# A fused graph, attention and expert kernel on one core: tiles and superchunks taken from the last to the first, x and its table moved tile by tile, two buffer sets for the permutation

## The reference, cut to what matters

```python
xn = layernorm(x)                                   # x: 6250 x 256
def sage(h, Wl, bl, Wr):
    agg = segment_sum(h[src], dst)                  # 100000 edges, dst sorted
    return agg / max(count(dst), 1) @ Wl.T + bl + h @ Wr.T
g   = sage(relu(sage(xn, W1l, b1, W1r)), W2l, b2, W2r)
x   = x + g + mix(xn)                               # linear attention over all nodes, two layer norms, a two-layer MLP
H   = gelu(layernorm(x) @ fW1 + fb1)                # 1024 wide
p   = softmax(H @ Wg + bg); e = argmax(p)           # 8 experts, top 1
out = x + p[e] * (H @ Wd[e] + bd[e])
```

## Time and profile before

| what | value |
|---|---|
| median of 3 runs | 2529.69 us (2522.98 to 2529.9) |
| the profiled execution's own time | 2532.22 us |
| its span | 2530.2 us |
| mean granted TensorE clock | 0.877 |
| busy PE, DVE, ACT, POOL | 77%, 45%, 22%, 66% |
| HBM traffic | 332.56 MB, mean 131 GB/s |

### The profile page before, as it was taken

One profiled execution on the slowest core, in us unless ns is written; L12 is line 12 of the kernel. 1 busy time (PEld: TensorE's weight loads), 2 busy tenths in 40 slices (PEclk: granted clock), 3 DMA queues, 4 the chain that ended last, 5 costly groups with the idle time before them and its releaser, 6 DMA issues.

```text
span 2530.2 us, 41380 instructions
## 1 busy us (share of the span) xinstructions
PE 1958.9 (77%) x9589; PEld 1205.7 (48%) x9590; DVE 1138.0 (45%) x3192; ACT 560.1 (22%) x1269; POOL 1673.8 (66%) x1749
## 2 busy tenths in 40 slices
PE   3566778878888898994344666778899999779998
PEld 1234445445555565662011233444455555468886
DVE  5522323347677777773212233334445555432222
ACT  6433334332222222220000000111122222201110
POOL 2677777777777777726777777777777776044442
PEclk9988888889899999997555677888999999889999
DMA  5444444444444444423343444445455544235551
GB/s 181 139 116 117 116 117 120 120 129 131 130 131 137 131 132 133 135 67 110 102 122 106 141 128 140 142 143 156 153 160 156 156 153 144 81 120 164 169 163 67
DMA packets 154316, 332.56 MB, mean 131 GB/s; under 512 B 34181, under 2 KB 88423, under 8 KB 154245
## 3 DMA queue, kind: packets, MB, share of 16 engines
q0 software_dynamic: 85824, 248.21, 33.6%
q10 hardware_dynamic: 42630, 58.35, 6.6%
q1 hardware_dynamic: 25794, 25.32, 3.1%
HBM read 273.97 MB, written 58.72 MB: 131 GB/s over the span
## 4 chain that ended last, share of the span: by engine, by line
POOL 34%; PE 33%; issue 15%; DMA 6%; DVE 4%; ACT 2%; POOLq 2%; ACTq 1%; DVEq 1%; SPq 1%
POOL big L647 34%; PE bank L517 10%; PE bank L1617 8%; PE bank L1387 6%; DMA mbuf<-qT_d 4%; PE bank L1605 2%; PE bank L1393 2%; PE bank L1542 1%; PE bank L1417 1%; PE bank L1484 1%; DMA big<-hh_d,edges 1%; POOLq L644 1%; PE bank L1412 1%; POOLq L642 1%; ACT big L1174 1%
## 5 line engine op out<-in xcount | busy, mean ns | idle before, releaser
L647 POOL DMA_INDIRECT big<-hh_d,edges x782 | 750.2, 959 | 291.1 <-issue 231.8
L647 POOL DMA_INDIRECT big<-xh_d,edges x782 | 771.7, 987 | 246.4 <-issue 234.0
L1387 PE MATMUL bank<-big,S 128*128 x1960 | 599.2, 431 | 267.0 <-SPq L583 260.5
L791 DVE SCALAR_TENSOR_TENSOR S<-edges,tv,iota 128x512 f16<-128x512 f16 x490 | 359.7, 752 | 480.8 <-PE bank L1387 349.8
L1387 PEld LDWEIGHTS bank<-big,S 128*128 128x128 f16 x1960 | 205.0, 105 | 559.7 <-issue 419.6
L1385 PE MATMUL bank<-ones,S 128*128 128x1 f16 x980 | 167.5, 171 | 109.8 <-SPq L583 107.9
L517 PE MATMUL bank<-turned,x1T 128*128 128x512 f32 x392 | 195.4, 621 | 0.0
L1385 PEld LDWEIGHTS bank<-ones,S 128*128 128x128 f16 x980 | 96.1, 98 | 126.2 <-SPq L583 120.6
L667 POOL DMA_INDIRECT out_dram<-big,node_s x56 | 57.0, 1018 | 145.5 <-DVE big L1123 145.5
L517 PE MATMUL bank<-turned,mbuf 128*128 128x512 f32 x196 | 110.5, 693 | 0.0
L517 PEld LDWEIGHTS bank<-turned,abuf 128*128 128x128 f32 x784 | 96.8, 195 | 24.0 <-issue 23.0
(11 more groups left out here) (217 smaller groups left out, 2936.0 us busy)
## 6 DMA issues: line engine op xcount, KB each, us to landing
hx_d<-mbuf ACTq DMA_DIRECT2D x49, 512.0 KB
big<-xh_d,edges POOLq DMA_INDIRECT x782
big<-hh_d,edges POOLq DMA_INDIRECT x782
big<-in_fwd_dram SPq DMA_DIRECT2D x8, 1024.0 KB
qT_d<-abuf ACTq DMA_DIRECT2D x49, 128.0 KB
hh_d<-HL ACTq DMA_DIRECT2D x49, 128.0 KB
mbuf<-qT_d ACTq DMA_DIRECT2D x49, 128.0 KB
hx_d<-res ACTq DMA_DIRECT2D x49, 128.0 KB
```

Of the source, the lines that this page charges most:

```text
L647: e.indirect_dma_start(G[:, r, n % SC, :], None, table, bass.IndirectOffsetOnAxis(ap=srcx[:, n:n + 1], axis=0)).then_inc(d_g[r], 16)
L791: VI.done(e.scalar_tensor_tensor(S[:, walk.u, :, :], dst[:, bass.ds(c * SC, SC)].unsqueeze(2).to_broadcast([P, SC, P]), tv[:, bass.ds(k, 1 ...
L1387: ins = e.matmul(AGG[:], S[:, walk.u, j, :], G[:, bass.ds(slot, 1), j, :].rearrange("p a c -> p (a c)"), start=False, stop=False, skip_gro ...
```

## The change

All tiles are handled from the last to the first: tile t of the program is now nodes (48 - t) * 128 onward (`rows`), superchunk c is now chunks (196 - c) * 4 onward, so superchunk 0 has no chunks, superchunk 1 has two, and the others four. The tables of items and `free_words`, the masks and every load and store of tiles follow. Items 0 to 97 now hold 28 finishes and 70 superchunks, items 98 to 244 hold 21 finishes and 127 superchunks (counted from the inputs). x is loaded tile by tile (49 loads; that of the partial tile waits for three GpSimd clears instead of one), and `xh_d` is stored tile by tile (49 stores instead of 21). GpSimd clears two pieces of the ring more, VectorE clears `xnS` once. The permutation's loop is written out, has two sets of `OL` and `RH` (the second `OL` lies in S), VectorE writes the tile part before the row part, and waits for TensorE's sum of two groups before.

```diff
+def rows(t):
+    return slice((TILES - 1 - t) * P, (TILES - t) * P)
...
-        OL = Gf[:, 0:GROUP * P].rearrange("p (t r) -> p t r", r=P)
-        RH = Gf[:, GROUP * P:GROUP * (P + 3 * SLOTS)].rearrange("p (t k s) -> p t k s", k=3, s=SLOTS)
+        OLS = [a[:, 0:GROUP * P].rearrange("p (t r) -> p t r", r=P)
+               for a in (Gf, S.rearrange("p a b c -> p (a b c)").bitcast(F32))]
+        RHS = [Gf[:, GROUP * (P + n * 3 * SLOTS):GROUP * (P + (n + 1) * 3 * SLOTS)].rearrange("p (t k s) -> p t k s", k=3, s=SLOTS)
+               for n in range(2)]
...
-        X_IN = 32
+        X_IN = 16 * GROUP
...
-        VP = Loop(sem("v_perm"), [x + h for h in "01" for x in ("row", "tile")])
+        VP = Loop(sem("v_perm"), [x + h for h in "01" for x in ("tile", "row")])
...
-                return self.kept((self.k + self.u - self.t) % 256, SUPER - 1)
+                return self.kept((self.t + (SUPER - 1 - self.u) - self.k) % 256, SUPER - 1)
...
-            return range(c * SC, min((c + 1) * SC, CHUNKS))
+            first = (SUPER - 1 - c) * SC
+            return range(min(first, CHUNKS), min(first + SC, CHUNKS))
...
+                for t in (*range(g * GROUP + 1, (g + 1) * GROUP), g * GROUP):
+                    if t > 0:
+                        e.dma_start(res[:, t, :], x[rows(t), :]).then_inc(d_x[g], 16)
+                    else:
+                        e.wait_ge(p_setup, 3)
+                        e.dma_start(res[0:LAST_ROWS, t, :], x[(TILES - 1) * P:N, :]).then_inc(d_x[g], 16)
...
-                    at = slice(g * (GROUP * P) + a * P, g * (GROUP * P) + b * P)
-                    e.dma_start(xh_d[at, :].rearrange("(t p) c -> p t c", p=P), xhl[:, a:b, :]).then_inc(d_xst[n], 16)
+                    for u in range(a, b):
+                        e.dma_start(xh_d[rows(g * GROUP + u), :], xhl[:, u, :]).then_inc(d_xst[n], 16)
...
-            e.memset(res[:, TILES - 1, :], 0.0).then_inc(p_setup, 1)
+            e.memset(res[:, 0, :], 0.0).then_inc(p_setup, 1)
+            for c in range(2):
+                rest = G[:, ring(0, c), len(chunks(c)):, :]
+                e.memset(rest.bitcast(F32), 0.0).then_inc(p_setup, 1)
...
+            step(e.memset(xnS, 0.0))
...
-                    if not first:
-                        PP.wait(e, f"sum{h}", g, 1)
+                    if g > 1:
+                        PP.wait(e, f"sum{h}", g, 2)
+                    VP.done(e.tensor_tensor(RH[:, a:b, 2, :], numbers(SLOTS), of(nv, SLOTS), ALU.is_equal), f"tile{h}")
                     VP.done(e.tensor_tensor(OL[:, a:b, :], numbers(P), of(mx, P), ALU.is_equal), f"row{h}")
-                    VP.done(e.tensor_tensor(RH[:, a:b, 2, :], numbers(SLOTS), of(nv, SLOTS), ALU.is_equal), f"tile{h}")
```

More of the change, by code:

```diff
@@ L581, in relay @@
             def relay(layer, c):
-                e.wait_ge(d_g[ring(layer, c)], landed(layer, c))
+                if landed(layer, c):
+                    e.wait_ge(d_g[ring(layer, c)], landed(layer, c))
                 e.sem_inc(s_ready, 1)
@@ L651, in _ @@
             e.wait_ge(d_sth, OPENED + 16 * TILES)
-            with e.Fori(0, TILES // GROUP) as g:
+            for g in range(TILES // GROUP):
+                RH = RHS[g % 2]
                 for h, (a, b) in enumerate(HALVES):
@@ L726, in moments @@
             def moments(g):
-                e.wait_ge(d_x[g], 32)
+                e.wait_ge(d_x[g], X_IN)
                 for i in range(g * GROUP, (g + 1) * GROUP):
@@ L1084, in _ @@
             rt(e.scalar_tensor_tensor(mx[:], nv[:], -float(P), mx[:], ALU.mult, ALU.add))
-            for first, g in turns(e, TILES // GROUP):
+            for g in range(TILES // GROUP):
+                OL, RH = OLS[g % 2], RHS[g % 2]
                 for h, (a, b) in enumerate(HALVES):
@@ L1194, in store @@
                     VB1.wait(e, "hlo", t)
-                    e.dma_start(hh_d[bass.ds(tile(e, t) * P, P), :], HL[:]).then_inc(d_h, 16)
+                    at = rows(t).start if isinstance(t, int) else within(e, (TILES - 1 + t.less) * P - t.base * P, (TILES - 1) * P)
+                    e.dma_start(hh_d[bass.ds(at, P), :], HL[:]).then_inc(d_h, 16)
                 def meanT(t):
@@ L1289, in turn_b @@
                 elif stage == 2:
-                    with e.If(i.base < TILES - 2):
+                    with e.If(i.base < TILES - 1):
                         next_loads(i)
-                    with e.If(i.base == TILES - 2):
-                        next_loads(i, True)
             turn_b(0, 0)
@@ L1588, in _ @@
             clear(FT[:, 0:3 * SLOTS])
-            with e.Fori(0, TILES // GROUP) as g:
+            for g in range(TILES // GROUP):
+                OL, RH = OLS[g % 2], RHS[g % 2]
                 for h, (a, b) in enumerate(HALVES):
+                    VP.wait(e, f"row{h}", g)
                     GP.wait(e, f"prob{h}", g)
```

59 lines of the change are left out of this document (26 added, 33 removed).

## The result

The changed kernel takes 2483.29 us (median of 4 runs, 2481.99 to 2484.57), the kernel before beside it 2529.8 us (4 runs, 2522.98 to 2531.23): a ratio of 0.9824 [0.9807, 0.9841], 46.5 us less. The forecast was 2481 us. The profiled execution has a span of 2480.7 us against 2530.2, 49.5 us less, and a mean granted clock of 0.881.

What follows compares the result with a forecast made beforehand. GpSimd's gathers were taken to pace both layers, with PE's backlog making the ends long. Start of layer 2 -19.7, layer 2 +1, its end -21.7 and permutation -8 sum to -48.4 us: 2481 us from 2529.69, range 2455 to 2513.

Steps and rivals of the forecast that it cites:

- What bounds the kernel: Both layers: GpSimd's gathers set the pace; TensorE holds them 12.7 us in 33 waits, all in layer 1.
- Prologue: Before the first gather: loading x in small pieces costs +2 us, with ends of -2 and +5.
- rival D: Prologue: 128 KB x loads at two thirds of 318 GB/s take 9 us more, time about 2490 us; chance 0.07.
- Stage A and the hold: Layer 1's first stage: PE's finishes hold the gathers 26 us (14 to 45); stage B's first item at 503.3 us.
- the change of stage: From stage A to stage B: 14.65 us in the trace, 8.5 us without the item and finish already priced.
- Rival B: Stage A: finishes cost less (4 us), so the hold is nearly 0 and the time 2456 us; chance 0.10.
- Layer 1 as a whole: Gathers of layer 1: 26 us of new hold come and 12.7 us of old waits go, +13.3 us.
- Between the layers: Last gather of layer 1 to first of layer 2: 18.5 us instead of 53.2.
- Rival C: Ends of the layers: something else than PE's backlog sets either, half of 56 us stays, 2510 us; chance 0.12.
- Layer 2: Gathers of layer 2 with light tiles first: the ring covers PE's loss, hold 1 us, ends 0 and 10.
- End of layer 2: Last gather to last logits: 2 + 35.2 + 2.5 us for the low clock, 39.7 us, 21.7 us less.
- Permutation: Permutation stage: two sets bring 33.1 us to 25.4, two groups at 4.3 us and five at 2.7; 8 us less.

Runs made afterwards that it cites:

- 3/2: The changed kernel with 3 items in a turn of stage A and 2 in one of stage B, instead of 2 and 3: 2468.2 us, ratio 0.9766.
- the other splits: The changed kernel with 3 and 2, or 1 and 4, items in a turn of stages A and B, instead of 2 and 3: 2468.2 and 2571.07 us.

## Why the prediction was right, and where it was not

The total was right within 2.3 us and the mechanism (the ends shrink, stage A pays) as well; the terms behind it were off in both directions, and the hold in stage A, 10.8 us, lies below the 14 to 45 us that the prediction gave it.

**What bounds the kernel.** GpSimd's pace, a gather per 1.26 us in layer 2 and per 1.30 us in layer 1, sets both layers: shown, since in 3/2 nothing held it and layer 1 is at 1014.0 us for 782 gathers. One reading was wrong: the prediction gave all 12.7 us of waits for PE to layer 1 and "nowhere in layer 2". The earlier trace rows hold both layers together; by layer it is 6.6 and 6.1 us, nearly all of it ordinary 0.30 us steps. Only 2.6 us of layer 1 were a real hold. So the 12.7 us to be gained there did not exist, and the 1.278 us a gather that I derived without them should have been (1012.3 - 2.6) / 782 = 1.291 us.

**Prologue:** +2 predicted, +2.7 measured, by the reason given (issue time on SP). The loads took longer than its 20 us (48 issues took 22.87 us), and 6.4 MB at 318 GB/s are 20 us and not 18. The rate did not hold, though the prediction expected it to: it fell to 272 GB/s in the changed kernel, by the pace of the issues, which is well above the two thirds of rival D. The Trainium skill's figure there (DMA: Bandwidth & Descriptors, "Measured", 138 GB/s for 64 KB, there for DMAs issued from GpSimd) would by the prediction's estimate have made it some 28 us more; the trace does not agree, with many pieces of 128 KB issued from SP.

**Stage A and the hold.** Predicted: the first item of stage B at 503.3 us, hold 26 us (14 to 45). Measured: 489.1 us and 10.8 us of hold. Stage A took 379.0 us from its first item to stage B's, 14.9 less than the 393.9 of the sum. Two terms make this up. A finish was taken as 5.05 us in every place. In the changed kernel a turn without one takes 4.98 us, 10 turns with a finish behind their first item 10.03 and 16 with one behind their second 9.4, and all 28 finishes cost 129.7 us, 4.63 each: 11.7 us less than priced. And the change of stage was counted in part twice. From the start of a turn's sum of keys and values to the next item it is 3.1 us, in which PE prepares the next tile; 49 turns of 4.98 us contain this 49 times, but the last turn has no next tile. (So the finishes are 370.7 us, the time to that sum at 480.8 us, less 244.0 for the turns and plus 3.1.) From the last such sum to the first item of stage B it is 8.3 us, most of it a wait for the queries:

```profile
488.12 1.22 PE L1498 MATMUL bank<-mbuf 128*128 128x132 f32 x4 [6.70 <-DMA mbuf<-qT_d]
```

So the 8.5 us were about right in size, and 3.1 us too much in the sum. The ends of the range do not come out of that sum either: with 4.5 and 5.6 us a finish it gives 10 and 41 us, not 14 and 45, and the measured hold lies just inside.

When the hold comes was wrong as well. The sum compares PE and GpSimd at the end of stage A; 8.7 of the 10.8 us came at 261 to 358 us, where PE needs some 24.4 us for two light tiles with their turns and GpSimd some 20 us for the gathers, and none from there to the boundary, where a tile has one superchunk more (two turns, 14.4 us, beside some 15 us of gathers). It did not end at the boundary: the rest came at 520 and 536 us, where a turn of stage B without a finish takes 7.3 to 9.7 us (7.2 in the earlier trace rows) and one with a finish up to 16. All waits for PE in layer 1, ordinary steps included, are 18.3 us, below the 20 to 35 that were to show the mechanism. Rival B (no hold) was nearer to the hold than the forecast.

**Layer 1 as a whole** nevertheless lost more than predicted, 19.9 instead of 13.3 us. Against before, 8.2 us are new hold and 11.7 us are longer gathers, a term that the sum didn't have: 226 gathers met a one-hot instead of 206, at 1.105 us each instead of 1.058. That VectorE's one-hots make gathers longer is what the run with doubled one-hots shows, and the excess of the gathers that met one covers the 11.7 us: (1.105 - 0.960) x 226 = 32.8 us against (1.058 - 0.961) x 206 = 20.0 us, 12.8 us more. Why a gather that meets one is dearer in the new order (what else runs beside it) stays open.

**Between the layers:** 18.5 predicted, 18.1 measured, and 17.9 and 18.3 in the other splits. From the last item's sum it is 14.8 us, where 14.0 and 2.5 for the clock were added. Rival C (the boundary stays) is refuted. First gather of layer 2: 1138.7, 12.5 us earlier instead of 19.7, nearly all of the difference from layer 1.

**Layer 2:** +1 predicted, -0.4 measured. Light tiles first are covered by the ring.

**End of layer 2:** 39.7 predicted, 34.4 measured. The step that failed is the extra 2.5 us for a low clock on top of the 35.2 us taken from before. From the last item's start to the last logits it is now 32.4 us. The granted clock by stretch, first of the changed kernel, then of the one before:

```profile
2128.00:2132.00 4.00, 3.61 (x16) 2.60 (x17) 0.97 (x2) 0.88 (x3) 0.00 (x0) 0.61 0.14 25
2132.00:2136.00 4.00, 4.00 (x12) 1.62 (x11) 2.38 (x12) 1.18 (x3) 0.00 (x0) 1.00 0.97 326
...
2175.00:2185.00 10.00, 9.99 (x40) 6.00 (x40) 3.46 (x17) 3.16 (x6) 0.00 (x0) 0.83 0.16 59
2185.00:2201.00 16.00, 14.57 (x69) 10.64 (x68) 0.54 (x4) 5.14 (x8) 0.00 (x0) 0.76 0.19 74
```

In the changed kernel the clock is 0.50 until PE's last item begins at 2128.39 us, 0.61 in 2128 to 2132, full from 2132 to 2150 and 0.88 up to 2161. The stretch of 35.2 us that was copied had a low clock of its own: 0.83 and 0.76 in its last 26 us. By these rows PE spends about 6 us at the lower level in the new stretch and about 11 us in the old one (estimated from the mean clocks), and at half speed that difference is 2.7 us, the 35.2 less 32.4. So the price for the low clock was added to a stretch that already contained a larger one. Why the clock fell in the old stretch, where PE was busy nearly throughout, isn't shown.

**Permutation:** 25.4 predicted, 21.8 measured, -11.3 and, alone, -10.1 us in the median. PE's clock was priced (two groups at 4.3 us); it is hidden, and the 2.9 us a group that VectorE and GpSimd need in turn set the pace. The prediction took rows that overlap as evidence against the lock; the ends of the rows, shown with the permutation alone, speak for it.

**Sum.** -19.7 + 1 - 21.7 - 8 = -48.4 predicted for the profiled execution, -49.5 measured. The errors cancelled: +7.2 us at the start of layer 2, -5.3 at the end, -3.3 in the permutation, +1.7 in the expert part and -1.4 in layer 2. The range would have held any of them; the agreement of the sum to a few microseconds is partly luck. The ends of the parts, all added, give about 2460 to 2520 us and not 2462 to 2510.

## What to carry to other kernels

Where one engine sets the pace and another one follows through a ring, put the follower's heavy work (here the many finishes of light tiles) early and its light work late: its backlog at the end is on the critical path, a backlog at the start is not, as long as the ring covers it. How much of the follower's work comes to one piece of the pacing engine's at the start is then a setting of its own: here a constant of 1, 2 or 3 items a turn moved the time from 2571 over 2483 to 2468 us with nothing else changed. Before a wait is priced from a group's total, count how many of its instances are longer than the ordinary step between two instructions. Before a stretch is copied from a trace and a price added to it, look whether the stretch already contains that price. And where two engines' rows overlap, look at their ends before you take it for overlapping work.

## What the runs showed of the hardware

- A gather of 128 rows on GpSimd's queue takes 0.95 us, and in layer 1 1.05 to 1.1 us where it meets a VectorE one-hot of 0.75 us (226 gathers at 1.105 against 556 at 0.960 in the changed kernel; in its layer 2 only 0.975 against 0.950). Doubling the one-hots of layer 2 made its 782 gathers 20 to 34 us longer.
- In the permutation VectorE's and GpSimd's operations on SBUF ended strictly in turn, each by a step of its own width behind the other's end (VectorE 0.56, 0.41, 0.25 and 0.19 us for 512, 384, 224 and 168 f32, GpSimd 0.42 and 0.33 us for 224 and 168). Their rows contain the wait: 0.65 us for a comparison that takes 0.39 us alone.
- 48 DMA issues of 128 KB from one queue took 0.476 us each, which set the rate: 272 to 278 GB/s, with the DMA engines busy for 0.83 to 0.91 of the time, against 318 GB/s with 896 KB pieces. The cost was that a small DMA behind them was issued 6.8 us later.
- The granted clock of TensorE was 0.50 over 76 us in which it was busy for 28.60 us, 0.61 over the 4 us in which steady work began (2128 to 2132 us) and 1.00 over the 4 us behind them.
- Two other chips ran the kernel before 25% longer. In a trace from there PE, VectorE and ScalarE have waits of 13 us and more that nothing in the profile ends. They lengthened the layers (the gap between them from 18 to 28 us in the order of the changed kernel) and not the permutation (21.8 to 22.0 us), so a ratio from there can't be read as one from an undisturbed chip.
